# The first four run products of a scan moved from the seventh place of a front loop to the sixth, with the splitting of B and u one place sooner

## The chip, the cores and the metric

The kernel runs on one core of one Trainium2 chip. The metric is the device time of one execution in microseconds (us); the value given is the median of three runs. Engines are called as the profile calls them: PE (TensorE matmuls) with PEld (its weight loads), DVE (VectorE), ACT (ScalarE), POOL (GpSimd) and SP (SyncE, which issues DMAs).

## The reference, cut to what matters

Eight sequences of 512 tokens go through a quantised embedding with a two-tap convolution, then a layer norm, a linear state-space scan with 4 heads of 64 states, and a feed-forward part. Only the embedding, the norm and the start of the scan are touched here.

```python
h = relu(conv(w_emb[x]))                # (8, 512, 128), causal, two taps
u = layernorm(h)
Bu = (u @ B).reshape(8, 512, 4, 64)
# x[t] = x[t-1] @ A + Bu[t] for every head, from init_states; computed by a scan
y = xnorm(x) @ C + u @ D                # xnorm: scaled by the largest |x| of the step
h = h + y
h = h + ffn(layernorm(h))               # attn_w, then per-chunk experts, then next_w
```

## The kernel before, in words

Each of the NB = 8 sequences ("batches" 0 to 7) is 512 tokens, laid out as 32 chunks of 16 steps. The scan works on groups of GB = 4 batches: group 0 is batches 0 to 3, group 1 is 4 to 7. The heads are held in NP = 2 halves (a = 0 and 1), each 128 states.

**The front loop.** Every engine runs its own version of a loop over places b = 0 to 9. In order, PE does at place b: `gather(b)` (16 bf16 matmuls of a one-hot matrix with the table, into bank 2; it waits until ACT has read bank 2 for the batch before), the spreading of the token ids of a later batch, `prepare` (matmuls that build powers of A and products of B with them, L1029), `transpose_u(b - 2)` (L1092), more `prepare`, at places 6 and 7 four `run_piece` calls of the scan, and from place 8 steps of the carry and `fuse`. ACT at place b: the relu that writes `h` of batch b (L614), copies of the prepared products (L570), the copy `uT` of the transposed batch b - 2 (L619), for some batches half of the normalisation of batch b - 1 (L631), then at place 6 `split_high`, and at places 6 and 7 `copy_runs`. DVE at place b: the statistics of batch b (L774, L778), then the normalised `u` of batch b - 1 (L807), then at place 6 the low parts of the split (L813, L814, L784). POOL turns the statistics of each batch into 1/std and shift (L483 to L486). So the life of one batch is: gather on PE, relu on ACT, statistics on DVE, 1/std on POOL, normalisation on DVE (and ACT) one place later, transposition on PE two places later.

**The run products.** `run_piece(g, n)` with a, q = divmod(n, 4) adds u of step q of every run of four steps, times B A^(3-q), into the bank of half a. Half 0 takes plain fp32 matmuls, two instructions each (L1106). Half 1 takes three fp32r products of high and low parts (L1112), which `split_high` on ACT (L603, L604, L606) and the subtractions on DVE prepare. Of group 0, the half a = 0 runs at place 6 and the half a = 1 at place 7. The copies out of the banks are `copy_runs(0, 0)` at place 6 and `copy_runs(0, 1)` at place 7. The run pieces of half 0 wait for `uT` of batches 0 to 3 (`uT_ready` at 4), written on ACT at places 2 to 5.

Every engine works through its program strictly in the order written, and waits on semaphores.

Of the kernel before, what the change touches and what calls it, by code (L numbers as in the profile page):

```python
# [45 lines left out]
NB = 8  # L46
# [4 lines left out]
GB = NB // NG  # L51
# [21 lines left out]
RUN = 4  # L73
# [25 lines left out]
def build(nc, ids, emb, conv, pack_a, pack_b, fc1, fc2, out):  # L99
    with ExitStack() as ctx:  # L100
# [3 lines left out]
        def sem(name):  # L104
            return ctx.enter_context(nc.semaphore(name))
# [112 lines left out]
        u_t_done, uT_ready = sem("u_t_done"), sem("uT_ready")  # L218
# [112 lines left out]

        PREP_ROUND = ((1, 0), (1, 0), (1, 0), (1, 1), (1, 1), (1, 2), (1, 1), (1, 1), (1, 1), (1, 0))

        FUSED_FRONT = 3
        MIXER = 8

# [20 lines left out]
        def numbered(plan):  # L357

            done, out = dict(fuse=FUSED_FRONT, run=RUN, carry=0, input=0, step=0), {}
            for j, places in plan.items():  # L360
# [50 lines left out]
        with nc.Block() as block:  # L411
# [25 lines left out]
            def _(pool):  # L437
# [65 lines left out]
                def fused_lo_of(e):  # L503

                    pool.wait_ge(fused_ready, e + 1)
                    pool.wait_ge(fused_full, e + 1 - FUSED_FRONT)
                    nc.gpsimd.tensor_tensor(out_p[1][:, e, :], fused_copy(), out_p[0][:, e, :].bitcast(F32),  # L507
                                            ALU.subtract).then_inc(fused_lo_pool, 1)

                for e in range(FUSED_FRONT, NE - 1):  # L510
                    fused_lo_of(e)
# [43 lines left out]
            def _(act):  # L555
# [22 lines left out]
                def copy_fused(e):  # L578
                    act.wait_ge(fused_done, e + 1)
                    nc.scalar.activation(out_p[0][:, e, :], fuse_bank(e)[:], ACT.Copy).then_inc(fused_ready, 1)  # L580
                    if e >= FUSED_FRONT:
                        if e > FUSED_FRONT:
                            act.wait_ge(fused_lo_pool, e - FUSED_FRONT)
# [18 lines left out]
                def split_high():  # L602
                    nc.scalar.activation(late_p[:, 0], late(1), ACT.Copy).then_inc(b_hi, 1)  # L603
                    nc.scalar.activation(b_p[:, 0], pa[:, PA["b"]], ACT.Copy).then_inc(b_hi, 1)  # L604
                    for b in range(GB):
                        nc.scalar.activation(u_split(0, 0)[:, b], uT[:, b], ACT.Copy).then_inc(u_hi[0], 1)  # L606

                act.wait_ge(ld_pa, 32)
                for b in range(NB + 2):
                    if b < NB:  # L610
                        act.wait_ge(gat_done, b + 1)
                        if b == 0:
                            act.wait_ge(scale_h_ready, 1)
                        nc.scalar.activation(h[:, b, :], bank[2][:], ACT.Relu, scale=scale_h[:]).then_inc(h_ready, 1)  # L614
                    for t in prep_tasks(b, 0):
                        copy_out_prep(t)
                    if b >= 2:
                        act.wait_ge(u_t_done, b - 1)
                        nc.scalar.activation(uT[:, b - 2, :, :].rearrange("p i k -> p (i k)"), bank[3][:],  # L619
                                             ACT.Copy).then_inc(uT_ready, 1)  # L620
                    for t in prep_tasks(b, 1):
                        copy_out_prep(t)
                    if 1 <= b <= NB and U_DVE[b - 1] < NQ:
                        act.wait_ge(rstd1_ready, b)
                        if b == 1:
                            act.wait_ge(h_ready, 1)
                        if b >= 3:
                            act.wait_ge(u_t_done, b - 2)
                        for q in range(U_DVE[b - 1], NQ):
                            s = slice(q * CH, (q + 1) * CH)  # L630
                            last = nc.scalar.activation(u[:, (b - 1) % 2, s], h[:, b - 1, s], ACT.Identity,  # L631
                                                        scale=rstd1[:, b - 1, q:q + 1], bias=shift1[:, b - 1, q:q + 1])
                        last.then_inc(u_act_ready, 1)
                    if b == NB - 2:
                        split_high()
                    if b in (NB - 2, NB - 1):
                        copy_runs(0, b - (NB - 2))
                    if b >= NB:
                        copy_fused(b - NB)
# [37 lines left out]
                for j in range(-3, NB):  # L677
                    for n in range(8):
# [26 lines left out]
                        b = j + 1  # L705
# [8 lines left out]
                        b = j + 2  # L714
# [8 lines left out]
            def _(dve):  # L723
# [64 lines left out]
                for b in range(NB + 1):  # L788
                    if b + 3 < NB:
                        one_hot(b + 3)  # L790
                    if b < NB:
                        dve.wait_ge(h_ready, b + 1)
                        statistics(b, st1, st1_ready, mv1, mv1_ready)
                    if b == NB:
                        dve.wait_ge(ld_pb, 16)
                        dve.wait_ge(ld_pa, 32)
                        nc.vector.tensor_scalar(attn_g[:], pb[:, PB["attn"]], pa[:, PA["ln_g"]], None,
                                                ALU.mult).then_inc(attn_g_ready, 1)
                        nc.vector.tensor_scalar(centre[:], ident, -1.0 / CH, None, ALU.add).then_inc(centre_ready, 1)
                    if b >= 1:  # L800

                        dve.wait_ge(rstd1_ready, b)
                        if b >= 3:
                            dve.wait_ge(u_t_done, b - 2)
                        for q in range(U_DVE[b - 1]):
                            s = slice(q * CH, (q + 1) * CH)
                            last = nc.vector.tensor_scalar(u[:, (b - 1) % 2, s], h[:, b - 1, s],  # L807
                                                           mv1[:, b - 1, q, 0:1], rstd1[:, b - 1, q:q + 1],
                                                           ALU.subtract, ALU.mult)
                        last.then_inc(u_ready, 1)  # L810
                    if b == NB - 2:
                        dve.wait_ge(b_hi, 2)
                        nc.vector.tensor_tensor(late_p[:, 1], late(1), late_p[:, 0].bitcast(F32), ALU.subtract).then_inc(b_lo, 1)  # L813
                        nc.vector.tensor_tensor(b_p[:, 1], pa[:, PA["b"]], b_p[:, 0].bitcast(F32), ALU.subtract).then_inc(b_lo, 1)  # L814
                        for n in range(GB):
                            split_low(0, n)
# [82 lines left out]
                for j in range(-3, NB + 1):  # L899
                    b = j + 1  # L900
# [21 lines left out]
                    b = j + 3  # L922
# [15 lines left out]
                    b = j + 1  # L938
# [14 lines left out]
                    b = j + 2  # L953
# [16 lines left out]
                    b = j + 3  # L970
# [47 lines left out]
            def _(pe):  # L1018
# [76 lines left out]
                def run_piece(g, n):  # L1095
                    a, q = divmod(n, RUN)
                    if n == 0:
                        pe.wait_ge(uT_ready, GB * (g + 1))
                        pe.wait_ge(prep_ready, N_LATE)
                    if q == 0 and g == 1:  # L1100
                        if a == 0:
                            pe.wait_ge(run_ready[0], 1)
                        else:
                            pe.wait_ge(x_ready[0], NP * (RUN - 1))
                    if a == 0:
                        last = mm(scan_bank(a), b_then(a, RUN - 1 - q), u_runs(g, q), start=(q == 0), stop=(q == RUN - 1))  # L1106
                    else:
                        if q == 0:
                            pe.wait_ge(b_lo, 2)
                            pe.wait_ge(u_lo[g], GB)  # L1110
                        for k, (w, m) in enumerate(PARTS):
                            last = mm(scan_bank(a), b_split(w, a, RUN - 1 - q), u_runs_split(g, m, q),  # L1112
                                      start=(q == 0 and k == 0), stop=(q == RUN - 1 and k == len(PARTS) - 1))
                    if q == RUN - 1:
                        last.then_inc(run_done[g], 1)
# [102 lines left out]
                for b in range(NB + 2):  # L1218
                    if b == 0:
                        pe.wait_ge(tab_ready, 1)  # L1220
                    if b < NB:
                        gather(b)
                    if 3 < b + 3 < NB:
                        spread_ids(b + 3)
                    for t in prep_tasks(b, 0):
                        prepare(t)
                    if b >= 2:
                        transpose_u(b - 2)
                    for t in prep_tasks(b, 1):
                        prepare(t)  # L1230
                    if b in (NB - 2, NB - 1):
                        for q in range(RUN):
                            run_piece(0, (b - (NB - 2)) * RUN + q)
                    if b >= NB:
                        carry_step(0, b - NB)
                        fuse(b - NB)
# [207 lines left out]
```

## Time and profile before

| | |
|---|---|
| median of 3 runs | 171.67 us (171.63 to 171.71) |
| the profiled execution, its own time | 171.82 us |
| its span, first to last instruction | 170.1 us |
| busy, share of the span | PE 95%, PEld 82%, DVE 75%, ACT 60%, POOL 60% |
| chain that ended last | PE 83%, ACT 5%, POOL 4%, DVE 3%, issue 3%, DMA 1% |
| granted TensorE clock | full in all 40 slices |

The profiled execution lies 0.15 us above the median, and 1.7 us of its time lie outside the span. The chain is followed back from the last instruction, at each step to whatever released it; it says which engine carried the time. Starts and durations of neighbouring instructions overlap slightly in a timeline, since engines are pipelined, so the distance between two starts is the better measure of what a piece of work costs its engine.

### The profile page before, as it was taken

How to read it: one execution, taken by the hardware profiler on the slowest of the kernel's cores; microseconds unless marked ns; L12 is line 12 of the kernel's file. 1: busy time of each engine (PE TensorE's matmuls, PEld its weight loads, DVE VectorE, ACT ScalarE, POOL GpSimd, SP SyncE). 2: the span in 40 equal slices, each digit the busy share in tenths (PEclk: the TensorE clock that was granted, in tenths of full speed). 3: DMA queues.
4: the chain of work that ended last, by engine and by line, in shares of the span. 5: the costliest groups of instructions: out<-in, count | busy, mean ns of one | idle time of the engine just before them, and what ended most of it. 6: DMA issues, size and time to landing. Idle time of an engine off the chain costs nothing.

```text
span 170.1 us, 3494 instructions
## 1 busy us (share of the span) xinstructions
PE 161.4 (95%) x1165; PEld 138.8 (82%) x1165; DVE 127.9 (75%) x403; ACT 102.1 (60%) x238; POOL 101.8 (60%) x168
## 2 busy tenths in 40 slices
PE   5988989999999999999999989999999999989992
PEld 1676875887766799987679889999999999979991
DVE  3969959833338384897994997989979898649883
ACT  3048999462134532423435857959779597788991
POOL 5337687669997035361313694996979969785000
PEclk9999999999999999999999999999999999999999
DMA  4996000000000000000000000010010100110022
GB/s 144 354 428 287 4 0 2 0 6 0 0 0 0 4 0 0 0 6 0 0 0 0 4 0 0 0 67 0 0 67 0 64 4 0 62 62 6 0 105 82
DMA packets 2182, 7.47 MB, mean 44 GB/s; under 512 B 238, under 2 KB 748, under 8 KB 1908
## 3 DMA queue, kind: packets, MB, share of 16 engines
q1 hardware_dynamic: 2146, 7.23, 11.2%
q8 instruction: 9, 0.15, 0.3%
q14 instruction: 9, 0.07, 0.1%
q10 hardware_dynamic: 18, 0.02, 0.1%
HBM read 5.15 MB, written 2.10 MB: 43 GB/s over the span
## 4 chain that ended last, share of the span: by engine, by line
PE 83%; ACT 5%; POOL 4%; DVE 3%; issue 3%; DMA 1%; POOLq 0%; ACTq 0%; DVEq 0%
PE bank L1347 12%; PE bank L1327 12%; PE bank L1276 8%; PE bank L1191 6%; PE bank L1185 5%; PE bank L1273 4%; PE bank L1056 4%; PE bank L1106 4%; PE bank L1081 4%; PE bank L1296 4%; PE bank L1112 3%; PE bank L1303 2%; POOL rstd L521 2%; PE bank L1029 2%; POOL hid_p L538 2%
## 5 line engine op out<-in xcount | busy, mean ns | idle before, releaser
L538 POOL TENSOR_TENSOR hid_p<-hid_f,hid_p 128x256 fp32r<-128x256 f32 x48 | 34.2, 736 | 13.6 <-ACT hid_p L696 13.6
L694 ACT ACTIVATE hid_f<-bank,pa 128x256 f32<-128x256 f32 x64 | 30.8, 492 | 16.0 <-PE bank L1327 14.1
L1327 PE MATMUL bank<-xaT_p,fc_p 128*128 128x256 f32 x192 | 35.1, 294 | 0.2 <-issue 0.2
L1347 PE MATMUL bank<-hid_p,out_hi 128*128 128x256 f32 x128 | 32.5, 290 | 1.0 <-POOL hid_p L538 1.0
L1327 PEld LDWEIGHTS bank<-xaT_p,fc_p 128*128 128x128 f32 x192 | 26.7, 190 | 0.4 <-issue 0.4
L1347 PEld LDWEIGHTS bank<-hid_p,out_hi 128*128 128x128 f32 x128 | 23.4, 188 | 2.0 <-POOL hid_p L538 1.4
L696 ACT ACTIVATE hid_p<-bank,pa 128x256 fp32r<-128x256 f32 x48 | 23.4, 488 | 0.0
L1276 PE MATMUL bank<-pb,xh 128*128 128x128 f32 x128 | 19.5, 275 | 0.0
L521 POOL TENSOR_TENSOR rstd<-spread,neg_half 128x8 f32<-128x8 f32 x8 | 13.6, 1697 | 9.5 <-DVE spread L966 9.5
L1347 PE MATMUL bank<-hid_p,out_lo 128*128 128x256 f32 x64 | 17.9, 279 | 0.0
L1276 PEld LDWEIGHTS bank<-pb,xh 128*128 128x128 f32 x128 | 16.9, 192 | 0.0
L774 DVE BATCH_NORM_STATS2 st<-h 128x6 f32<-128x128 f32 x64 | 13.9, 280 | 3.1 <-ACT h L614 2.8
L594 ACT ACTIVATE X<-bank 128x512 f32<-128x512 f32 x12 | 7.2, 598 | 14.6 <-PE bank L1191 14.6
L507 POOL TENSOR_TENSOR out_lo<-hid_f,out_hi 128x512 fp32r<-128x512 f32 x5 | 6.4, 1275 | 14.1 <-ACT hid_f L584 14.1
L946 DVE SCALAR_TENSOR_TENSOR xaT_p<-bank,attn_c,xaT_p 128x256 fp32r<-128x256 f32 x16 | 7.0, 479 | 8.1 <-ACT xaT_p L710 8.1
L1191 PE MATMUL bank<-X,pa 128*128 128x512 f32 x24 | 12.7, 610 | 0.0
L1273 PE MATMUL bank<-pb,uT 128*128 128x128 f32 x64 | 12.5, 277 | 0.0
L931 DVE TRANSPOSE_TENSOR_REDUCE amax<-X 128x16 f32<-128x512 f32 x16 | 10.4, 687 | 2.7 <-ACT X L594 2.7
L1347 PEld LDWEIGHTS bank<-hid_p,out_lo 128*128 128x128 f32 x64 | 12.1, 189 | 0.0
L580 ACT ACTIVATE out_hi<-bank 128x512 fp32r<-128x512 f32 x8 | 4.8, 598 | 11.8 <-PE bank L1056 11.8
L1081 PEld LDWEIGHTS bank<-tab,onehot 125*128 125x128 bf16 x128 | 8.8, 107 | 3.0 <-issue 2.5
L918 DVE TENSOR_SCALAR xa<-bank,rstd,shift 128x128 f32<-128x128 f32 x32 | 10.9, 404 | 0.3
(161 smaller groups left out, 375.7 us busy)
## 6 DMA issues: line engine op xcount, KB each, us to landing
fc_w<-in_fc SPq DMA_DIRECT2D x2, 2048.0 KB, 11.4
out<-res SPq DMA_DIRECT2D x7, 256.0 KB, 2.0
pa<-in_pack_a SPq DMA_DIRECT2D x1, 407.0 KB, 3.2
pb<-in_pack_b SPq DMA_DIRECT2D x1, 384.0 KB, 4.5
out<-res SPq DMA_DIRECT2D x2, 128.0 KB, 1.7
pw<-in_pack_a SPq DMA_DIRECT2D x1, 64.0 KB, 3.1
emb_w<-in_emb SPq DMA_DIRECT2D x1, 62.5 KB
conv_w<-in_conv ACTq DMA_DIRECT2D x1, 1.0 KB
```

The costliest lines, as they stand in the source:

```text
L521: nc.gpsimd.tensor_tensor(rstd2[:, b, :, :].rearrange("p s q -> p (s q)"), spread2[:, b % 2, :, :].rearrange("p s q -> p (s q)"), neg_half[:],
L538: nc.gpsimd.tensor_tensor(hid_p[1][:, half, c, :], hid_f[:, m % HID_SLOTS, :], hid_p[0][:, half, c, :].bitcast(F32), ALU.subtract).then_in ...
L694: full = nc.scalar.activation(hid_f[:, m % HID_SLOTS, :], src, ACT.Gelu, bias=bias)
L696: nc.scalar.activation(hid_p[0][:, half, c, :], src, ACT.Gelu, bias=bias).then_inc(hid_ready, 1)
L774: last = nc.vector.bn_stats(st[:, b % 2, q, :], h[:, b, q * CH:(q + 1) * CH])
L918: last = nc.vector.tensor_scalar(xa[:, s], bank[4][:, s], rstd2[:, b, 1, q:q + 1], shift2[:, b % 2, q:q + 1], ALU.mult, ALU.subtract)
L1081: last = mm(bank[2][:, q * CH:(q + 1) * CH], onehot[:, b % OH_SLOTS, at:at + P], tab[:, part, tap, :], start=(n == 0), stop=(n == 3))
L1191: mm(scan_bank(a), a1, every_run(g, a, q), start=False, stop=True).then_inc(state_done[g], 1)
L1273: mm(dst, uT[:, b, q * TQ:(q + 1) * TQ, :].rearrange("p i k -> p (i k)"), pb[:, PB["d"]], start=True, stop=False)
L1276: last = mm(dst, xh[:, b % 2, a, q * P:(q + 1) * P], pb[:, PB["c"]][:, a * CH:(a + 1) * CH], start=False, stop=(a == NP - 1))
L1327: last = mm(fc1_bank(8 * b + n)[:, 0:HALF], fc1_p[w][:, e * HID + c * P:e * HID + (c + 1) * P], xaT_p[m][:, b % 2, half, :], start=(k == 0 ...
L1347: last = mm(out_bank(b, half)[:, half * HALF:(half + 1) * HALF], out_p[w][:, e, c * CH:(c + 1) * CH], hid_p[m][:, half, c, :], start=(c == ...
```

## The change

A tuple `FIRST_RUNS = (NB - 3, NB - 1)`, that is (5, 7), says at which places PE issues the first and the second half of group 0's run products. Before, these were places 6 and 7. The first half (four run pieces, eight matmul instructions) thus moves from behind place 6's work to behind place 5's, which is ahead of `gather(6)`, the seventh gather. The second half stays at place 7. The splitting of B and of u on ACT and DVE moves from place 6 to place 5. ACT's `split_high` gets a wait for `uT` of batch 3, which ACT itself wrote earlier in the same place. The copies `copy_runs` stay at places 6 and 7. No instruction of work is added or removed.

```diff
+        FIRST_RUNS = (NB - 3, NB - 1)
@@ split_high, on ACT
                     nc.scalar.activation(b_p[:, 0], pa[:, PA["b"]], ACT.Copy).then_inc(b_hi, 1)
+                    act.wait_ge(uT_ready, GB)
                     for b in range(GB):
@@ ACT, front loop
-                    if b == NB - 2:
+                    if b == FIRST_RUNS[0]:
                         split_high()
                     if b in (NB - 2, NB - 1):
                         copy_runs(0, b - (NB - 2))
@@ DVE, front loop
-                    if b == NB - 2:
+                    if b == FIRST_RUNS[0]:
                         dve.wait_ge(b_hi, 2)
@@ PE, front loop
-                    if b in (NB - 2, NB - 1):
+                    if b in FIRST_RUNS:
                         for q in range(RUN):
-                            run_piece(0, (b - (NB - 2)) * RUN + q)
+                            run_piece(0, FIRST_RUNS.index(b) * RUN + q)
```

## Rows read from the trace of the kernel before

**Rows 1.** The page, its parts 1 and 4: busy time, chain
```profile
PE 161.4 (95%) x1165; PEld 138.8 (82%) x1165; DVE 127.9 (75%) x403; ACT 102.1 (60%) x238; POOL 101.8 (60%) x168
...
PE 83%; ACT 5%; POOL 4%; DVE 3%; issue 3%; DMA 1%; POOLq 0%; ACTq 0%; DVEq 0%
```

**Rows 2.** Busy time by stretch: span, each engine, PEclk, DMA share, GB/s
```profile
0.00:9.00 9.00, 7.15 (x30) 4.10 (x31) 5.94 (x17) 1.90 (x3) 3.81 (x22) 1.00 0.75 257
...
23.25:30.15 6.90, 6.85 (x52) 4.58 (x50) 5.73 (x24) 6.48 (x16) 5.19 (x8) 1.00 0.00 1
30.15:37.03 6.88, 6.88 (x44) 6.19 (x42) 4.55 (x20) 2.85 (x9) 3.94 (x8) 1.00 0.01 4
```

**Rows 3.** Timeline of PE: start, us, engine line op, names, shapes, idle before
```profile
21.74 0.63 PE L1092 MATMUL bank<-ident_m,u 128*128 128x128 f32 x4 [0.27 <-DVE u L807]
...
23.25 1.06 PE L1081 MATMUL bank<-tab,onehot 125*128 125x128 bf16 x16
...
25.33 2.74 PE L1106 MATMUL bank<-uT,late_b 128*128 128x512 f32 x6
...
28.77 1.06 PE L1081 MATMUL bank<-tab,onehot 125*128 125x128 bf16 x16
...
30.15 0.60 PE L1092 MATMUL bank<-ident_m,u 128*128 128x128 f32 x4
...
30.80 2.35 PE L1112 MATMUL bank<-u_first,late_p 128*128 128x512 f32 x9
...
37.03 0.60 PE L1092 MATMUL bank<-ident_m,u 128*128 128x128 f32 x4
```

**Rows 4.** Timeline of DVE, the same columns
```profile
20.98 0.57 DVE L807 TENSOR_SCALAR u<-h,mv,rstd 128x128 f32<-128x128 f32 x2
...
25.16 0.87 DVE L774 BATCH_NORM_STATS2 st<-h 128x6 f32<-128x128 f32 x4 [1.14 <-ACT h L614]
...
26.36 1.08 DVE L807 TENSOR_SCALAR u<-h,mv,rstd 128x128 f32<-128x128 f32 x4
27.36 0.55 DVE L813 TENSOR_TENSOR late_p<-late_b,late_p 128x384 fp32r<-128x384 f32 x1
...
28.17 2.49 DVE L784 TENSOR_TENSOR u_first<-uT,u_first 128x512 fp32r<-128x512 f32 x4
30.59 0.87 DVE L774 BATCH_NORM_STATS2 st<-h 128x6 f32<-128x128 f32 x4
...
33.96 1.12 DVE L807 TENSOR_SCALAR u<-h,mv,rstd 128x128 f32<-128x128 f32 x4 [0.75 <-POOL shift L486]
...
51.59 3.70 DVE L784 TENSOR_TENSOR hid_p<-uT,hid_p 128x512 fp32r<-128x512 f32 x4 [1.37 <-POOL hid_p L501]
```

**Rows 5.** Timeline of ACT, the same columns
```profile
22.40 0.60 ACT L619 ACTIVATE uT<-bank 128x512 f32<-128x512 f32 x1
...
23.67 0.87 ACT L631 ACTIVATE u<-h,shift,rstd 128x128 f32<-128x128 f32 x2
24.44 0.68 ACT L614 ACTIVATE h<-bank,scale_h 128x512 f32<-128x512 f32 x1
...
25.80 0.27 ACT L570 ACTIVATE pk_t<-bank 128x128 f32<-128x128 f32 x1
25.96 0.52 ACT L603 ACTIVATE late_p<-late_b 128x384 fp32r<-128x384 f32 x1
26.37 0.42 ACT L604 ACTIVATE b_p<-pa 128x256 fp32r<-128x256 f32 x1
26.68 2.18 ACT L606 ACTIVATE u_first<-uT 128x512 fp32r<-128x512 f32 x4
```

**Rows 6.** Timeline of POOL, the same columns
```profile
25.34 0.24 POOL L486 TENSOR_SCALAR shift<-tmp 128x4 f32<-128x4 f32 x1
...
27.96 2.75 POOL L485 TENSOR_TENSOR tmp<-mv,rstd 128x4 f32<-128x4 f32 x1
```

**Rows 7.** Waits of PE over the whole span: us in total, times, longest
```profile
PE bank L1347 <- POOL hid_p L538: 1.0, 2, 0.5
...
PE bank L1139 <- ACT pw L570: 0.3, 1, 0.3
```

## The prediction, made before the changed kernel was run

> **What bounds the kernel now.** I read the chain and the busy shares first, then the busy time of the stretch that the change touches, then the timelines of the four engines across it. The page shows PE busy for 95% of the span and on 83% of the chain [rows 1]: time can come only from PE's gaps, and any new gap in PE is lost unless something later gives it back. The stretches say where gaps are. From 23.25, where the seventh gather starts, to 30.15 PE is busy 6.85 of 6.90 us, and from there to 37.03 it is busy 6.88 of 6.88 [rows 2]. So in the two places across which work is moved there are some 0.05 us to win, and everything else that the change can do is a loss or nothing. The waits agree: behind this stretch the first one of PE is 0.3 us for a copied power (L1139), and the largest total is 1.0 us for POOL's low parts far behind [rows 7].
>
> **How the order stands.** PE: seventh gather (batch 6) at 23.25, a table product, transposition of batch 4, a table product, then the four run pieces of half 0 from 25.33 until the eighth gather (batch 7) at 28.77, then a table product, transposition of batch 5 at 30.15, and half 1 from 30.80 [rows 3]. Six of the eight half 0 matmuls stand in the row shown; the pieces cost PE 28.77 - 25.33 = **3.44 us** from start to start. DVE: statistics of batch 6 at 25.16, after 1.14 us of waiting for its h, then u of batch 5 at 26.36 for 1.08 us (ending at 27.44), then the split's subtractions from 27.36 to 30.66, and only then the statistics of batch 7 at 30.59 [rows 4]. What matters: DVE's u of batch 5 is written behind the statistics of batch 6, and these need the gather of batch 6. PE uses u of batch 5 at 30.15, so it has 30.15 - 27.44 = 2.71 us. A DVE result reached PE 0.19 us after its end in the one case where PE was waiting for it (u ended at 20.98 + 0.57 = 21.55, the transposition began at 21.74 [rows 3, 4]), so the free slack is 2.71 - 0.19 = **2.52 us**.
>
> **Part 1: the run pieces ahead of the seventh gather.** Up to 23.25 nothing changes. They need uT of batch 3, which ACT writes from 22.40 to 23.00 [rows 5]; the first weight load would fall some 0.1 us ahead of 23.25, so a wait here is about 0 (bounds 0 to 0.1). PE then does the same work in another order: pieces 23.25 to 26.69, seventh gather at 26.69 (3.44 later than before), and the table products and transposition of batch 4 fill the time so that the eighth gather would again start at 28.77. It needs h of batch 6 read out of the bank: before, this read began 24.44 - 23.25 = 1.19 after the gather's start and took 0.68 [rows 3, 5], so now it ends at 26.69 + 1.19 + 0.68 = 28.56, just in time (0.2 before the gather). The table product behind it needs a copy that ACT finished at 25.80 + 0.27 = 26.07 [rows 5]; 3.44 later that is 29.51, and PE wants it about 29.6. Both margins are thin, but a miss of a tenth or two there costs nothing of its own, because of the next wait.
>
> **Where the stall goes.** h of batch 6 ends 3.44 later, and with it the statistics start at 25.16 + 3.44 = 28.60 and u of batch 5 at 26.36 + 3.44 = 29.80, ending at 30.88. PE can transpose it at 30.88 + 0.19 = 31.07, and stands ready at 30.15. **New gap: 31.07 - 30.15 = 0.92 us**, which is the same as 3.44 less the slack of 2.52. Queued behind the waiting transposition on PE are the table product, half 1 of the runs and all that follows, so the whole rest of PE's program moves by it.
>
> **Part 2: the split one place sooner.** On ACT it is 2.90 us (25.96 to 28.86 [rows 5]). Now it starts when the normalisation of batch 4 is done, at 24.44 where h of batch 6 was before, and ends at 27.34; the h of batch 6 is wanted from 26.69 + 1.19 = 27.88, so it hides in the time in which ACT waits for the gather (cover 0.54 us; beyond that each tenth would delay the statistics by a tenth). The added wait for uT of batch 3 is on ACT's own copy, ended at 23.00: nothing. On DVE the subtractions cost 30.59 - 27.36 = 3.23 us [rows 4]. They start when both high parts of B are written, at 24.44 + 0.41 + 0.42 = 25.27; a signal from ACT reached DVE in 0.04 (h ended at 24.44 + 0.68 = 25.12, the statistics began at 25.16), so they begin at 25.31 and end at about 25.31 + 3.23 = 28.54. The statistics of batch 6 are ready for DVE at 28.60. This is nearly even, so the split costs 0 to 0.1. What it gives back: before, it stood ahead of the statistics of batch 7; now these start behind u of batch 5 at about 30.8 instead of 30.59, so its u comes 0.2 us later than 33.96 + 1.12 = 35.08, at 35.3, and is transposed at 37.03 + 0.92 [rows 3, 4]: no new wait. Half 1 would find its parts at 28.6 rather than 30.66, but it was not waiting for them: it began at 30.80 in a PE without a gap [rows 2, 3].
>
> One thing of POOL bears on the sum. Its small product L485 took 2.75 us from 27.96 to 30.71, just until DVE's subtractions were over [rows 4, 6], beside 0.24 for its equally small neighbour. The Trainium skill (GPSIMD Engine Reference, Key points) says that POOL shares its SBUF interfaces with VectorE, with contention when the DVE instruction has two SBUF inputs; the row agrees. By the rows alone: POOL's last step for batch 5 starts at 25.34 [rows 6], and the moved subtractions begin at 25.31. If they catch it, it ends near 28.6 + 0.24 = 28.9, still ahead of 29.80, where u of batch 5 wants it. So the sum stays at 0.92, with 0.9 us of room on that side.
>
> **The sum.** Gap 0.92, other parts 0 with bounds -0.05 (the only idle time of the stretch) and +0.2 (copy of uT, late split). The profiled execution of 171.82 would become 172.74; against the median of 171.67, 0.15 lower, **172.6 us**. Is it given back later? PE waits behind this stretch for ACT's power copy, which stands behind the copy of a product that PE has just made, and for POOL's low parts [rows 7], which are made from PE's own fc1 results. These move with PE. POOL's splitting of fc1 moves only 0.2 us, since it starts behind the last u (35.08), and nothing of PE was seen waiting for it.
>
> **The rivals.**
> - **A, the gap as worked out: 172.6 us**, with 172.3 to 172.9 for the bounds and a few tenths that a shift in phase between POOL and PE may give or take. Chance 0.76.
> - **B, a longer split.** DVE's four subtractions take 2.49 us at 28.17 but 3.70 us at 51.59, where POOL copies beside them [rows 4]. If the moved ones run at that rate, the statistics of batch 6 start 1.2 us later, and all of it passes to PE: 0.92 + 1.2 = 2.1, 173.8 us. Against it: POOL has little to do between 25.6 and the statistics of batch 6. A part of this, some tenths, is likelier than all. Chance 0.09.
> - **C, not slower: the gap is taken back.** For this the later waits of PE would have to be for something that does not move with it. It decides at 0.92 us: 0.3 at L1139 and 1.0 at L1347 [rows 7] would have to shrink by nearly that, leaving 171.7 us. For it: POOL is an engine with its own backlog there, and it moves by 0.2 at first. Against it: these operands are made from PE's products. Chance 0.08, with under 0.2% either way the likely form.
> - **D, the change misses its mark.** The runs move, but something keeps the chain of batch 6 early, so that u of batch 5 is in time; then there are 0.05 us of gap to win and the time is 171.6 us. It needs 0.92 us less than the 3.44 us of the run pieces between gather and statistics; the program order on PE (pieces, then gather) and on DVE (statistics, then u) allows no such path. Chance 0.04.
> - **E, the clock falls.** The row of the first 9 us has PE idle for 1.85 us in gaps and the granted clock at 1.00 [rows 2]; so a gap of 0.92 us should not lower it. If it did, the first nine matmuls of half 1 alone, 2.35 us [rows 3], would take about twice as long: 171.67 + 0.92 + 2.35 = 174.9 us or more. Chance 0.03. The Trainium skill (TensorE: Matmul & The Clock Gate, Part 1) says that a PE left idle is put back to 1.2 GHz, which speaks against opening a gap; here the first 9 us do not show it.
>
> **How the numbers follow.** Likeliest is A, 172.6 us. The range must leave out no more than 2 in 10: it takes A whole, the smaller form of B, and the nearer part of C: 172.1 to 173.2 us. What this kernel's measurement can tell from no change is about 0.2%, or 0.34 us: under 171.33 is faster, over 172.01 slower. A, B and E are slower, 0.88; C and D are split between the same (0.08) and faster (0.04).
>
> **What would show it right or wrong.** Right: in the changed trace the transposition of batch 5 has a gap of about 0.9 us before it that DVE's u (L807) ends, the statistics of batch 6 stand near 28.6, POOL's L485 is not stretched for batch 6, and PE's starts behind are later by the same 0.9 everywhere. Wrong in size: the statistics start when DVE's last subtraction ends and not when h is there (B), or the gather itself waits. Wrong in kind: no gap at that transposition (D), or a gap there but shorter waits at L1139 and L1347 and an unmoved end (C), or a granted clock under 1.00 (E).

## The result, and the profile after

Both kernels ran five times beside each other: 172.37 us (172.02 to 172.85) for the changed kernel, 171.68 us (171.63 to 171.72) for the one before. The ratio is 1.0041, with a 95% interval of 1.0028 to 1.0054. So the change makes the kernel slower, by 0.69 us, where 172.6 us and 0.92 us were forecast. The profiled execution took 172.37 us with a span of 170.6 us (170.1 before).

In the changed kernel the lines are shifted by two or three: the gather is L1084, the table products L1032, the transpositions of u L1095, the run pieces of half 0 L1109 and of half 1 L1115, the normalisation L810, the statistics L777, the subtractions L816, L817 and L787. The timeline of PE across the two places (start, us, engine line op, names, shapes, idle time before):

```profile
22.44 0.67 PE L1032 MATMUL bank<-pw,pw_t 128*128 128x256 f32 x2 [0.16 <-ACT pw_t L572]
22.94 0.38 PE L1032 MATMUL bank<-pw_t,pw 128*128 128x128 f32 x2
23.16 2.74 PE L1109 MATMUL bank<-uT,late_b 128*128 128x512 f32 x6
25.74 1.02 PE L1109 MATMUL bank<-uT,pa 128*128 128x512 f32 x2
26.60 1.06 PE L1084 MATMUL bank<-tab,onehot 125*128 125x128 bf16 x16
27.50 0.44 PE L1032 MATMUL bank<-pw,pw_t 128*128 128x128 f32 x2
27.77 0.60 PE L1095 MATMUL bank<-ident_m,u 128*128 128x128 f32 x4
28.21 0.39 PE L1032 MATMUL bank<-pw_t,pw 128*128 128x128 f32 x2
28.53 1.05 PE L1084 MATMUL bank<-tab,onehot 125*128 125x128 bf16 x16
29.42 0.65 PE L1032 MATMUL bank<-pw,pk_t 128*128 128x256 f32 x2
30.76 0.66 PE L1095 MATMUL bank<-ident_m,u 128*128 128x128 f32 x4 [0.69 <-DVE u L810]
31.25 0.39 PE L1032 MATMUL bank<-pk_t,pw 128*128 128x128 f32 x2
31.40 2.38 PE L1115 MATMUL bank<-u_first,late_p 128*128 128x512 f32 x9
...
35.20 1.49 PE L1128 MATMUL bank<-X,pw 128*128 128x248 f32 x6
```

There is one new gap, 0.69 us ahead of the transposition of batch 5, ended by DVE's u. Before, this transposition stood at 30.15 without a gap [rows 3]. All times of this profile lie 0.09 us earlier up to the table product at 22.44, which nothing of the change touches: DVE's half of u of batch 3, which the transposition just ahead of it reads, stands at 20.89 here and at 20.98 before [rows 4]. Counted from that product, which I use as the zero of all comparisons below (22.53 before), the transposition of batch 5 moved from 7.62 to 8.32 us, by **0.70 us**. Half 1 of the runs moved by 0.69 and the first carry product (L1128, 35.20) by 0.70, and from the carry product to the end of the span it is 135.4 us, against 135.5 before.

DVE in the same stretch:

```profile
25.20 0.56 DVE L816 TENSOR_TENSOR late_p<-late_b,late_p 128x384 fp32r<-128x384 f32 x1 [1.26 <-ACT b_p L606]
25.68 0.42 DVE L817 TENSOR_TENSOR b_p<-pa,b_p 128x256 fp32r<-128x256 f32 x1
26.01 2.49 DVE L787 TENSOR_TENSOR u_first<-uT,u_first 128x512 fp32r<-128x512 f32 x4
28.42 0.87 DVE L777 BATCH_NORM_STATS2 st<-h 128x6 f32<-128x128 f32 x4
29.32 0.38 DVE L781 BATCH_NORM_AGGREGATE mv<-st 128x2 f32<-128x6 f32 x4
29.62 1.08 DVE L810 TENSOR_SCALAR u<-h,mv,rstd 128x128 f32<-128x128 f32 x4
```

And the chain that ended last, as it comes to the gap (start, us, what):

```profile
24.45 0.41 ACT late_p L605
24.86 0.32 ACT b_p L606
25.18 0.02 issue
25.20 0.56 DVE late_p L816
25.76 0.33 DVE b_p L817
26.09 2.41 DVE u_first L787 x4
28.50 0.80 DVE st L777 x4
...
29.71 1.01 DVE u L810 x4
30.71 0.04 issue
30.76 0.66 PE bank L1095 x4
```

Before, the chain stayed on PE through this stretch; now it leaves PE for ACT's split, DVE's subtractions, the statistics of batch 6 and u of batch 5. The statistics show no idle time before them: DVE came to them when its subtractions were done. The relu that they also need:

```profile
27.70 0.69 ACT L617 ACTIVATE h<-bank,scale_h 128x512 f32<-128x512 f32 x1 [0.45 <-PE bank L1084]
```

It ended at 28.39, 0.03 us ahead of the statistics' start; the subtractions ended at 28.50 by their rows, which overlap their successor a little. So two limits stood side by side within 0.1 us: the delayed gather and the moved split. One profile can't say which of them costs the time, since with either gone the other would remain.

### The profile page after: what moved, and what is told of

It reads as the page before. It is cut to its first block, busy times and chain, and to the rows that moved or that the text cites. A ratio compares the mean times of both kernels' runs of the same rounds, so it can differ in the third digit from the quotient of the medians.

```text
span 170.6 us, 3494 instructions
## 1 busy us (share of the span) xinstructions
PE 161.0 (94%) x1165; PEld 138.1 (81%) x1165; DVE 127.9 (75%) x403; ACT 101.7 (60%) x238; POOL 99.4 (58%) x168
## 4 chain that ended last, share of the span: by engine, by line
PE 77%; ACT 6%; POOL 5%; DVE 5%; issue 3%; DMA 1%; POOLq 0%; ACTq 0%; DVEq 0%
PE bank L1350 12%; PE bank L1330 12%; PE bank L1279 8%; PE bank L1194 6%; PE bank L1188 5%; PE bank L1276 4%; PE bank L1059 4%; PE bank L1299 4%; PE bank L1115 3%; PE bank L1306 2%; POOL rstd L523 2%; PE bank L1109 2%; ACT u L634 2%; POOL hid_p L540 2%; PE bank L1160 2%
## 5 line engine op out<-in xcount | busy, mean ns | idle before, releaser
L777 DVE BATCH_NORM_STATS2 st<-h 128x6 f32<-128x128 f32 x64 | 13.9, 280 | 2.1 <-ACT h L617 1.9
L1276 PEld LDWEIGHTS bank<-pb,uT 128*128 128x128 f32 x64 | 10.0, 191 | 1.4 <-issue 1.0
```

The costliest lines, as they stand in the source:

```text
L777: last = nc.vector.bn_stats(st[:, b % 2, q, :], h[:, b, q * CH:(q + 1) * CH])
L1276: mm(dst, uT[:, b, q * TQ:(q + 1) * TQ, :].rearrange("p i k -> p (i k)"), pb[:, PB["d"]], start=True, stop=False)
```

## The experiments

Each was run beside the kernel before on the same chip. Executions of one kernel scatter more there than in the first comparison (those of the kernel before from 171.2 to 172.3 us), so the stretch in the trace is given beside each time.

### The changed kernel once more

> The changed kernel once more, as the control of this group. Both theories: 172.4 us, 0.4% over the kernel before, with a gap of about 0.7 us in PE ahead of the transposition of batch 5. Open: its five runs lay between 172.0 and 172.9 us, those of the kernel before within 0.1; if that comes from the gap itself, the scatter returns here and is absent wherever the gap is.

172.45 us (172.02 to 173.08), ratio 1.0035 (1.0019 to 1.0050). The gap is again 0.69 us, and the transposition of batch 5 stands 30.51 - 22.18 = 8.33 us from the zero. The scatter is not from the gap: the kernel before scatters in the same way there. In the profiles the scatter lies mostly ahead of the zero. DVE's first instruction, which waits for a DMA, begins at 2.07 us in the profile of before and at 2.61 in that of the next experiment. From the zero to the end of the span it is 147.6 us in the kernel before, and 148.2, 148.3 and 148.3 in the first profile of the changed kernel, in this one and in that of the next experiment, while their whole spans lie between 170.5 and 171.2.

### The split alone, and the run pieces alone

The split alone: the kernel before with

```diff
-                    if b == NB - 2:
+                    if b == NB - 3:
                         split_high()
@@ and the same for the subtractions on DVE; the wait for uT in split_high
```

> The split of B and u at place 5, the run pieces left at places 6 and 7. Theory S (two limits that are level: the delayed gather and DVE's subtractions each hold the statistics of batch 6 until 28.4 to 28.6): ACT is held by the split until 27.3, so h of batch 6 ends near 28.0 instead of 25.1, DVE's subtractions end near 28.5, and the statistics of batch 6 start there; the same gap of 0.7 to 0.9 us ahead of the transposition of batch 5, 172.3 to 172.6 us. Theory G (the gather behind the run pieces alone makes the gap): no gap, 171.7 us.

172.63 us (171.96 to 172.94), ratio 1.0040 (1.0021 to 1.0059). Theory S held. Its PE and DVE, with lines shifted by one:

```profile
22.90 0.67 PE L1030 MATMUL bank<-pw,pw_t 128*128 128x256 f32 x2 [0.16 <-ACT pw_t L570]
...
31.23 0.65 PE L1093 MATMUL bank<-ident_m,u 128*128 128x128 f32 x4 [0.54 <-DVE u L808]
```
```profile
26.48 2.49 DVE L785 TENSOR_TENSOR u_first<-uT,u_first 128x512 fp32r<-128x512 f32 x4
28.89 0.86 DVE L775 BATCH_NORM_STATS2 st<-h 128x6 f32<-128x128 f32 x4
```

The run pieces are where they were and the gather of batch 6 is early, yet the transposition of batch 5 stands 31.23 - 22.90 = 8.33 us from the zero, as in the changed kernel.

The run pieces alone: the changed kernel with the split back at place 6 on ACT and DVE.

```diff
-                    if b == FIRST_RUNS[0]:
+                    if b == NB - 2:
                         split_high()
@@ and the same for the subtractions on DVE
```

> The run pieces of half 0 at place 5, the split left at place 6. Theory S and theory G: the same gap of 0.7 us ahead of the transposition of batch 5, since the gather alone puts the statistics of batch 6 at 28.4; in addition half 1 of the runs waits for DVE's subtractions, which then stand behind u of batch 5 and end at 30.7 + 3.2 = 33.9 instead of 31.4 at PE: 2.5 us more, about 174.9 us. Theory D (the moved subtractions on DVE alone make the gap): no gap at the transposition, and the wait of half 1 alone, about 174.2 us.

176.72 us (174.76 to 177.56), ratio 1.0246 (1.0194 to 1.0298; it leaves out the longest of the four executions); the profiled execution took 174.76 us. PE and DVE of it:

```profile
22.14 0.67 PE L1032 MATMUL bank<-pw,pw_t 128*128 128x256 f32 x2 [0.16 <-ACT pw_t L572]
...
30.46 0.66 PE L1095 MATMUL bank<-ident_m,u 128*128 128x128 f32 x4 [0.69 <-DVE u L810]
...
33.76 2.35 PE L1115 MATMUL bank<-u_first,late_p 128*128 128x512 f32 x9 [2.42 <-DVE u_first L787]
```
```profile
28.12 0.87 DVE L777 BATCH_NORM_STATS2 st<-h 128x6 f32<-128x128 f32 x4 [4.48 <-ACT h L617]
```

Again 30.46 - 22.14 = 8.32 us. Here DVE stood idle for 4.48 us until h came. The statistics start 5.98 us from the zero in this kernel (held by the gather), 5.99 in the split alone (held by the subtractions) and 5.98 in the changed kernel. Each part of the change makes the whole gap by itself, and together they don't make it larger. Theories G and D, that one of them alone is the cause, both fall. The 2.42 us wait of half 1 is the part of the change that the early split avoids. The profiled time came out as worked out (174.9); the median did not, which the last experiment takes up.

### The order on DVE exchanged

The changed kernel, with u of batch 5 ahead of the statistics of batch 6:

```diff
-                    if b < NB:
+                    if b < NB and b != NB - 2:
                         dve.wait_ge(h_ready, b + 1)
                         statistics(b, st1, st1_ready, mv1, mv1_ready)
@@ behind the normalisation of batch b - 1
+                    if b == NB - 2:
+                        dve.wait_ge(h_ready, b + 1)
+                        statistics(b, st1, st1_ready, mv1, mv1_ready)
```

> The changed kernel with one exchange on DVE: at place 6 u of batch 5 stands ahead of the statistics of batch 6. Theory of the prediction (u of batch 5 is late only because it is written behind the statistics, which wait for the moved gather): u of batch 5 runs 28.4 to 29.5, PE finds it ready at about 29.9, no gap there, and the time is that of the kernel before, 171.6 to 171.8 us. Rival (the loss is in PE's new order or in contention, and would move elsewhere): 172.2 us or more, with another gap behind.

171.86 us (171.33 to 172.29), ratio 1.0005 (0.9989 to 1.0021). The gap is gone, and with it the loss, within that interval. Its PE, with lines shifted by three more:

```profile
22.24 0.67 PE L1035 MATMUL bank<-pw,pw_t 128*128 128x256 f32 x2 [0.16 <-ACT pw_t L572]
...
29.72 0.60 PE L1098 MATMUL bank<-ident_m,u 128*128 128x128 f32 x4
...
33.78 0.66 PE L1098 MATMUL bank<-ident_m,u 128*128 128x128 f32 x4 [0.18 <-DVE u L810]
...
34.50 1.42 PE L1131 MATMUL bank<-X,pw 128*128 128x248 f32 x6
```

The transposition of batch 5 stands at 7.48 from the zero (8.32 in the changed kernel, 7.62 before). I had not seen the small new gap of 0.18 us ahead of the transposition of batch 6: its statistics come 1.0 us later (29.25 - 22.24 = 7.01 from the zero, not 5.98), and POOL's 1/std behind them. So the first carry product stands at 12.26, against 12.06 before and 12.76 in the changed kernel: 0.50 of the 0.70 us are back.

### The pieces moved forward, but behind the gather

The kernel before with

```diff
                     if b < NB:
                         gather(b)
+                    if b == NB - 2:
+                        for q in range(RUN):
+                            run_piece(0, q)
@@ half 1 stays at place 7; ACT's split_high right behind the relu of batch 6
```

> The kernel before with the four run pieces of half 0 right behind the seventh gather instead of ahead of it (1.9 us later than in the changed kernel), and ACT's split right behind the relu of batch 6. Theory of the prediction: h of batch 6 comes as early as before, u of batch 5 near 27.5, no gap, 171.7 us. Rival (moving the pieces forward costs by itself, wherever they stand): a gap of some tenths and 172 us or more.

171.62 us (171.26 to 172.05), ratio 0.9991 (0.9979 to 1.0003), and no gap at the transposition of batch 5: it starts at 29.48 - 22.10 = 7.38 from the zero, and the first carry product at 12.05 (12.06 before). Moving the pieces forward costs nothing that can be told here; it also brings nothing. PE and DVE of it:

```profile
29.48 0.60 PE L1093 MATMUL bank<-ident_m,u 128*128 128x128 f32 x4
...
30.36 2.35 PE L1113 MATMUL bank<-u_first,late_p 128*128 128x512 f32 x9
```
```profile
27.73 2.49 DVE L785 TENSOR_TENSOR u_first<-uT,u_first 128x512 fp32r<-128x512 f32 x4
```

The transposition of batch 5 comes 0.24 us sooner than before (7.38, not 7.62), because that of batch 4 no longer waits for its input; why there was something to win is said in the next part. Half 1 then begins at 8.26, as before (8.27), and not 0.24 sooner: DVE's subtractions, which end at 27.73 + 2.49 = 30.22, are now what it finds last, 0.14 us ahead of its start.

### Filling the gaps that PE does have

The kernel before, with half of the first fused product in the gaps of place 5, and the second one ahead of the carry step of place 9:

```diff
+                    if b == NB - 3:
+                        fuse_piece(0, 0)
                     if b >= 2:
                         transpose_u(b - 2)
+                    if b == NB - 3:
+                        fuse_piece(0, 1)
...
-                    if b >= NB:
-                        carry_step(0, b - NB)
-                        fuse(b - NB)
+                    if b == NB:
+                        carry_step(0, 0)
+                        fuse_piece(0, 2)
+                        fuse_piece(0, 3)
+                    if b == NB + 1:
+                        fuse(1)
+                        carry_step(0, 1)
```

> An attempt at a better version: the kernel before, with two of the four pieces of the first fused product (0.22 us each) put into the two gaps of PE at place 5 (0.27 us ahead of the transposition of batch 3 and 0.16 us behind it), and at place 9 the second fused product ahead of the carry step that waited 0.29 us. If PE alone sets the time from there on, its gaps turn into time: 0.4 + 0.3 us less, 171.0 to 171.3 us. Rival (the chain of the batches sets the pace at place 5, and the carry chain behind place 9): the gaps only move, 171.6 us or more.

**170.62 us** (170.28 to 170.93), ratio 0.9935 (0.9919 to 0.9950): faster than both kernels, and by more than I had expected (171.0 to 171.3). PE there:

```profile
21.18 0.39 PE L1056 MATMUL bank<-pb,fc_w 128*128 128x128 f32 x2
21.61 0.63 PE L1092 MATMUL bank<-ident_m,u 128*128 128x128 f32 x4
22.07 0.39 PE L1056 MATMUL bank<-pb,fc_w 128*128 128x128 f32 x2
22.40 0.67 PE L1029 MATMUL bank<-pw,pw_t 128*128 128x256 f32 x2
...
36.90 1.06 PE L1056 MATMUL bank<-pb,fc_w 128*128 128x128 f32 x8
37.79 0.95 PE L1139 MATMUL bank<-X,pw 128*128 128x192 f32 x6
```

Neither filled gap shows idle time now. By the starts, what is left of the first fused product at place 8 takes 0.44 us (35.79 to 36.23) in place of 0.90, and at place 9 the second one (36.90 to 37.79) fills the time in which PE had waited. That wait had been more than the 0.29 us that its row showed: the transposition started at 37.03 [rows 3], takes 0.44 from start to start, and the carry step began at 37.91, so 0.44 us were free. The two come to 0.9 us. From the zero (22.40 here) to the end of the span it is 146.5 us against 147.6 before, so 1.1 of the 1.2 us between the medians lie behind the zero; what makes up the other 0.2 of them was not traced.

The same filling in the changed kernel with u of batch 5 first:

> The changed kernel with u of batch 5 ahead of the statistics of batch 6 on DVE and the same filling of gaps. If PE alone sets the time: 171.0 to 171.3 us, as the filled kernel before. Rival: with PE 0.4 us earlier the slack of u of batch 5 (about 0.4 us) is used up, and a gap of 0.1 to 0.3 us is left: 171.3 to 171.5 us.

170.76 us (170.52 to 171.29), ratio 0.9945 (0.9929 to 0.9961): no gap at batch 5, but one of 0.17 us at batch 6, as in the kernel with u first. With the gaps filled, moving the runs and the split forward brings nothing that can be told from the filled kernel before.

### Why the runs alone took more than worked out

> The runs-only kernel once more: its profiled execution took 174.8 us, as worked out, but its other executions lay between 176.5 and 177.6 us, at a mean granted clock of 0.981 to 0.989 against 0.997 of the profiled one. Theory C (with PE idle for 0.7 and 2.4 us within 4 us, some executions lose TensorE's full clock for a while): most executions again at 176 to 178 us with a clock under 0.99, and where the profile catches one, a stretch with PEclk under 1.00 behind the gap of half 1. Rival (scatter of the start, as in the other kernels): 174.5 to 175.5 us, clock 0.995 or more.

> The runs-only kernel with ten matmuls on zeros (bf16, 512 columns) put ahead of half 1 of the runs, where PE otherwise waits 2.4 us for DVE's subtractions. They take some 2.2 us, so PE works through the wait and nothing is later. Theory C (the clock is lost in the gap): all executions at 174.6 to 175.2 us with a clock of 0.995 or more. Rival (the extra time of the executions of 176 to 178 us is from something other than PE's idleness): the same 176 to 178 us here.

The runs-only kernel took 176.93 us this time (174.99 to 177.99), ratio 1.0265 (1.0197 to 1.0334; again without the longest execution), and now the profile, of an execution of 177.46 us, holds the cause. Busy time by stretch (span; busy time of PE, PEld, DVE, ACT, POOL; PEclk, the granted clock as a share of the full one; DMA share; GB/s), then PE:

```profile
32.00:34.00 2.00, 0.00 (x0) 0.02 (x1) 2.00 (x6) 1.94 (x5) 1.92 (x1) 0.66 0.00 0
34.00:36.00 2.00, 1.99 (x5) 1.61 (x6) 1.97 (x13) 0.00 (x0) 1.01 (x3) 0.50 0.03 8
36.00:38.00 2.00, 2.00 (x7) 1.51 (x6) 1.25 (x7) 0.00 (x0) 0.94 (x3) 0.50 0.00 0
38.00:40.00 2.00, 2.00 (x10) 1.71 (x9) 0.26 (x1) 0.49 (x2) 1.19 (x2) 0.64 0.01 4
```
```profile
34.01 4.18 PE L1115 MATMUL bank<-u_first,late_p 128*128 128x512 f32 x9 [2.42 <-DVE u_first L787]
37.99 1.48 PE L1115 MATMUL bank<-u_first,b_p 128*128 128x512 f32 x3
```

After gaps of 0.69 and 2.42 us the granted clock fell to its lower level, 1.2 GHz in place of 2.4, from within the second gap until near 39. The nine matmuls of half 1 that took 2.35 us in the other profile took 4.18, and from the start of half 1 to the first carry product it is 6.23 us (34.01 to 40.24) in place of 3.79 (33.76 to 37.55): 2.44 us for the clock. With ten matmuls on zeros ahead of half 1

```diff
+                    if b == NB - 1:
+                        for _ in range(10):
+                            mm(bank[7][:].rearrange("p (n m) -> p n m", n=NQ), zeros[:], ...)
```

the wait is as long, but PE is busy in it (2.32 us of matmuls, 0.26 us idle). All four executions then lay between 174.78 and 175.63 us, with clocks of 0.998 and 1.000 over the span, against 0.981 to 0.998 without; PEclk is 1.00 in every 2 us stretch from 28 to 46. So it is PE's idleness that loses the clock. Against the median with the busy wait, 175.13 us, the six executions with a clock under 0.99 are 1.3 to 2.9 us longer. The rule of the Trainium skill that was a rival in the prediction (TensorE: Matmul & The Clock Gate, Part 1: an idle PE is put back to 1.2 GHz) is thus seen in this kernel, in the gap of 2.42 us that follows one of 0.69, in six of eight executions, and not at the 0.69 us of the change alone. Whether the 2.42 us would do it without the gap ahead of it was not tried. In the changed kernel PEclk is 1.00 in every stretch up to 168 us; its mean of 0.998 comes from the last stretch, behind the last matmul.

## Why the prediction was right, point by point

One line of ACT in the kernel before that is needed below, its half of the normalisation of batch 3:

```profile
20.76 0.87 ACT L631 ACTIVATE u<-h,shift,rstd 128x128 f32<-128x128 f32 x2
```

- **What bounds the kernel.** Right that there was nothing for this change to win: no variant that moves only the run products and the split came out ahead of the kernel before, and the filling of gaps did. But "some 0.05 us to win" was read from busy shares, and the starts show more. Before, the distance from the table product of place 6 to the transposition of batch 4 is 24.64 - 24.15 = 0.49 us; in the changed kernel it is 27.77 - 27.50 = 0.27. So PE stood 0.22 us waiting there, for ACT's half of u of batch 4, which ended at 23.67 + 0.87 = 24.54 [rows 5]. The changed kernel and the one with the pieces behind the gather win it at that place, and lose it again at the waits behind it.
- **Part 1, the path through batch 6.** The run pieces cost 26.60 - 23.16 = 3.44 us, as worked out. The relu began 1.10 us behind the gather's start, not 1.19, so h came 0.09 earlier than in the sum. In the row that gave 1.19 the relu stood behind ACT's half of u of batch 4 (until 24.54 by its row) and had no idle time before it, so what it measured was ACT's order and not the path from the gather.
- **The gap, forecast 0.92, shift found 0.70.** The 0.22 us are in two terms: that 0.09, and the signal from DVE to PE, which I took at 0.19 from one row and which was 30.76 - 30.70 = 0.06. The 0.19 was a misreading. `transpose_u` waits for DVE's part of u and for ACT's (`u_ready` and `u_act_ready`), and of batch 3, from which I took it, ACT normalises half. This half (the line above) ended at 21.63, later than DVE's half (21.55) and 0.11 us ahead of the transposition at 21.74, though the profile puts that wait down to DVE. From batch 5 on DVE writes u alone. The gap by the starts is 0.85 (30.76 less 29.42 + 0.49), because PE also came there 0.15 us sooner: of the 0.22 us won at the transposition of batch 4, 0.10 were lost ahead of the eighth gather (28.53 - 28.21 = 0.32 us from the start of the table product, 0.22 before), and some hundredths lie between. That does not move the end, since u of batch 5 sets it.
- **Part 2, the split.** Its sizes were right (3.22 us of DVE, from 25.20 to 28.42), but its standing was not: I booked the gap to the gather and the split at "0 to 0.1". The chain names the split as the later of the two, by about 0.1 us, and alone it costs the full 0.70. That the number came out near from one limit alone is luck: both lay at the same place. Had I asked what remains with the runs left alone, the table of starts (25.31 + 3.23 = 28.54 beside 28.60) would have answered it.
- **POOL.** The step of batch 5 that met the subtractions took 0.61 us (25.25 to 25.86) and was not held to their end, so the 0.9 us of room was not used. For batch 6 the 2.75 us hold was absent, as expected.
- **What follows.** Right: nothing is given back. 135.4 us from the first carry product to the end, 135.5 before; the waits at the power copy (0.3) and at POOL's low parts (1.0) are unchanged [rows 7].
- **The rivals.** B did not happen: the four subtractions took 2.49 us, as before. Yet the sign that I had set for it, statistics that start when the last subtraction ends, was seen; it can't tell a longer split from one that is level with h. C and D are excluded by the traces. E did not happen in the changed kernel, whose executions show clocks of 0.995 to 1.000, and did in the runs-only one.

## What to carry to other kernels

When work is moved ahead on a full engine, follow the operation that it now precedes through every engine's program order to its next use on the full engine, and compare the delay with the slack at that use; and when two things are moved, work out each alone, for a gap can have two causes of which each suffices. Program order is often the cheap cure: an operation whose inputs are long ready should not stand behind one that waits for the moved work. On a bound engine look for gaps of a few tenths and for work that is ready early, and measure a gap by the distance of starts, since the idle time shown can be smaller than what is free. Take a delay between two engines only from a row in which the second had idle time and waited for the first alone; both terms that were mis-sized here came from rows that a third operation held up.

## What the runs showed of the hardware

- TensorE's clock: with gaps of 0.69 and 2.42 us within 4 us the full clock was lost in six of the eight executions of the runs-only kernel (means 0.981 to 0.989), for 6 to 7 us where the profile caught it; in the four executions with the second gap filled it was not (0.998 and 1.000).
- POOL beside DVE's subtractions with two inputs in SBUF: a POOL product of two tensors (L485 before, L487 in the runs-only kernel) that started within them was held until they ended (2.75 us from 27.96 in the kernel before [rows 6], and 2.75 us from 30.92 in the runs-only kernel, whose subtractions ended at 33.61). A product with a constant that started 0.05 us behind their first one took 0.61 in place of 0.24 us: it ended 0.10 us behind that first one (25.86 and 25.76) and was not held to the end of the others.
- From the end of DVE's row to the start of the transposition that waited for it alone: 0.05 to 0.06 us in the changed kernel (twice), the split alone, the runs alone and the kernel with u first. From the end of ACT's half of u of batch 3 to its transposition: 0.11 us in the kernel before, 0.10 in the changed one (21.55 to 21.65).
